# TensorE multiplies zeros in four of its pauses, and the first rows of the attention are scaled in another order

## The reference, cut to what matters

```
x = x + 0.5 * ffn(layernorm(x))       # router, top 2 of 64 experts, plus a shared expert
x = x + attn(layernorm(x))
x = x + 0.5 * ffn(layernorm(x))       # the same weights again

attn(x): n  = ln(x)*g + b
         W1 = gelu(n@h1_w1+b)@h1_w2+b;  W2 = gelu(n@h2_w1+b)@h2_w2+b
         W3 = tril(W1 @ W2^T);          t  = ln(gelu(W3 @ n))*g + b
         out = x + mlp_fm(ln(x + t)*g + b)
```

## Time and profile before

| | us |
|---|---|
| runs | 2206.85, 2216.04, 2218.53 |
| median | 2216.04 |
| profiled execution | 2217.58 |
| its span, first to last instruction | 2215.4 |
| PE busy | 1978.3 (89%) |
| DVE, ACT, POOL busy | 1324.0, 1085.1, 1105.9 |
| TensorE clock granted, mean of the span | 0.965 of full |

### The profile page before, as it was taken

How to read it: one execution, slowest core, us unless ns; L and a number is a source line. 1 busy time by engine, 2 the same in 40 slices (tenths; PEclk the granted TensorE clock), 3 DMA queues, 4 the chain that set the end, 5 groups by cost and what they waited for, 6 DMA issues and landing times.

```text
span 2215.4 us, 32427 instructions
## 1 busy us (share of the span) xinstructions
PE 1978.3 (89%) x11044; PEld 1675.5 (76%) x11044; DVE 1324.0 (60%) x3515; ACT 1085.1 (49%) x1988; POOL 1105.9 (50%) x1202
## 2 busy tenths in 40 slices
PE   6886888779999999999999999999999972888887
PEld 4665788658888888888888878878888862887754
DVE  6996555355576566576576575565565442554467
ACT  6774666434454454454454354444453442555643
POOL 5665666453245545545545645645525316555500
PEclk9998999989999999999999999999999985999999
DMA  8433888792032021121121210110100202888778
GB/s 274 144 105 129 269 272 275 245 301 61 1 96 67 30 95 38 59 95 41 56 89 31 73 43 21 52 39 20 58 10 20 86 10 67 274 274 287 240 250 280
DMA packets 236405, 270.06 MB, mean 122 GB/s; under 512 B 25489, under 2 KB 186322, under 8 KB 236242
## 3 DMA queue, kind: packets, MB, share of 16 engines
q1 hardware_dynamic: 199122, 192.40, 27.7%
q0 software_dynamic: 28672, 67.22, 9.3%
q10 hardware_dynamic: 8448, 8.39, 1.1%
HBM read 150.35 MB, written 117.57 MB: 121 GB/s over the span
## 4 chain that ended last, share of the span: by engine, by line
PE 60%; DVE 8%; issue 5%; ACT 4%; POOL 1%; DMA 1%; another core or an unknown queue 1%; SPq 0%; ACTq 0%; DVEq 0%; POOLq 0%
PE attention_ring L1926 20%; PE attention_acc L1956 13%; PE attention_acc L1946 8%; DVE attention_hid_l L1659 2%; PE attention_work L2016 2%; PE attention_work L1999 2%; PE attention_work L2032 2%; PE attention_work L2036 2%; PE attention_acc L2139 2%; PE attention_ring L2129 2%; PE attention_ring L2165 2%; PE attention_acc L2129 1%; PE attention_work L1914 1%; PE attention_ring L2116 1%; PE attention_work L1973 1%
## 5 line engine op out<-in xcount | busy, mean ns | idle before, releaser
L1659 DVE TENSOR_TENSOR attention_hid_l<-attention_gelu,attention_hid_h 128x512 fp32r<-128x512 f32 x384 | 284.5, 741 | 504.4 <-ACT attention_gelu L1303 320.3
L1300 ACT ACTIVATE attention_hid_h<-attention_ring,home_b 128x512 fp32r<-128x512 f32 x384 | 264.2, 688 | 572.6 <-PE attention_ring L1926 500.0
L1303 ACT ACTIVATE attention_gelu<-attention_ring,home_b 128x512 f32<-128x512 f32 x384 | 261.7, 682 | 0.0
L1956 PE MATMUL attention_acc<-attention_hid_h,home_w_h 128*128 128x512 f32 x512 | 203.9, 398 | 21.0 <-DVE home_room L1685 18.7
L1926 PE MATMUL attention_ring<-attention_n_t_h,home_w_h 128*128 128x512 f32 x512 | 206.0, 402 | 1.4 <-DVE attention_n_t_l L1651 1.4
L1926 PE MATMUL attention_ring<-attention_n_t_l,home_w_h 128*128 128x512 f32 x512 | 201.7, 394 | 0.0
L1926 PE MATMUL attention_ring<-attention_n_t_h,home_w_l 128*128 128x512 f32 x512 | 201.6, 394 | 0.0
L1956 PE MATMUL attention_acc<-attention_hid_l,home_w_h 128*128 128x512 f32 x512 | 200.3, 391 | 0.0
L1956 PE MATMUL attention_acc<-attention_hid_h,home_w_l 128*128 128x512 f32 x512 | 200.2, 391 | 0.0
L1147 POOL DMA_INDIRECT home_room<-expert_rows,routing_slots x128 | 135.9, 1061 | 98.3 <-issue 53.8
L648 POOL DMA_INDIRECT experts_xg<-xn_rows,routing_affine x128 | 141.8, 1108 | 71.9 <-PE experts_ps_t L741 35.3
(11 more groups left out here) (277 smaller groups left out, 5247.1 us busy)
## 6 DMA issues: line engine op xcount, KB each, us to landing
experts_w<-in_L_ffn_w SPq DMA_DIRECT2D x64, 256.0 KB
expert_rows<-experts_y SPq DMA_DIRECT2D x64, 256.0 KB
slot_rows<-const_zeros SPq DMA_DIRECT2D x16, 1024.0 KB
token_rows<-const_zeros SPq DMA_DIRECT2D x16, 1024.0 KB
home_room<-in_L_ffn_w SPq DMA_DIRECT2D x64, 256.0 KB
home_room<-slot_rows SPq DMA_DIRECT2D x64, 256.0 KB
final_y_rows<-token_rows SPq DMA_DIRECT2D x32, 512.0 KB, 7.4
dispatch_x_in<-in_L_attn_x SPq DMA_DIRECT2D x16, 512.0 KB, 7.1
```

What stands on the lines that cost most here:

```text
L1300: act.activation(hid[n % PARTS][0][:, :], ring[n % RING][:, :], ACT.Gelu, bias=b1[:, m, c:c + 1])
L1303: act.activation(gelu[n % GELUS][:, :], ring[n % RING][:, :], ACT.Gelu, bias=b1[:, m, c:c + 1]).then_inc(ring_free, 1)
L1659: dve.tensor_tensor(hid[n % PARTS][1][:, :], gelu[n % GELUS][:, :], hid[n % PARTS][0][:, :].bitcast(fp32), ALU.subtract).then_inc(hid_read ...
L1956: last = pe.matmul(acc[e % 3][:, :], w2[m][wp][:, c, k * P:(k + 1) * P], hid[s][xp][:, :], start=(c == 0 and q == 0), stop=(c == FC - 1 an ...
```

## The change

It has two parts.

**A multiplication of zeros.** A new function issues matmuls of the constant tile (128 columns of it as weights, all 256 as data) into a bank of PSUM whose content nobody needs at that time. PE calls it in four places: 60 times at the start of `experts`, ahead of `turn(0)`; 30 times at the start of the attention, after a new wait for `x_ready` 2; 90 times after the last `down`, ahead of `turn_x`; 165 times after the last placing, ahead of the first slots. The wait of L2142 moves ahead of the 90.

**The start of the attention.** ACT gets one activation with Gelu on 128 single numbers as its first instruction there. DVE makes `n` of group 0 before `z`, now with a wait for `x_scales` ahead of `n_first`. `n_second(0)` no longer waits for `z_ready`, and POOL's `sums` does instead.

```
+def keep_turning(pe, out, zeros, times):
+    for _ in range(times):
+        pe.matmul(out, zeros[:, 0:P], zeros[:, :], start=True, stop=True)
...
@@ experts, tensor
+            keep_turning(pe, ps_y[1][:, 0, :], consts["zeros"], 60)
             turn(0)
             turn(1)
...
@@ attention_to_end, gpsimd, sums(j)
                 pool.wait_ge(n_ready, 8 * (j + 1))
+                pool.wait_ge(z_ready, GT * (j + 1))
...
@@ scalar
+            act.activation(table_in[:, :], consts["partition"][:, :], ACT.Gelu)
...
@@ vector, n_second(j)
-                dve.wait_ge(z_ready, GT * (j + 1))
+                if j:
+                    dve.wait_ge(z_ready, GT * (j + 1))
...
             row_statistics(0)
-            make_z(0)
+            dve.wait_ge(x_scales, 1)
             n_first(0)
             n_second(0)
+            make_z(0)
             turned_lo(0, TURN_M, n_t, 0, n_hi, n_lo)
...
@@ tensor
+            pe.wait_ge(x_ready, 2)
+            keep_turning(pe, acc[2][:, 0:D], consts["zeros"], 30)
             pe.wait_ge(n_ready, 8)
             turn(n_of(0), None, 0)
...
+            pe.wait_ge(ring_free, item(HALVES, FC - 1) + 1)
+            keep_turning(pe, ring[2][:, 0:D], consts["zeros"], 90)
             turn_x(HALVES + 1, (place_in_done, x_turned), (HALVES - 1, KD * (HALVES - 1)))
             router(HALVES + 1)
             place_tiles(HALVES + 1, index_done, GT * HALVES)
+            keep_turning(pe, ring[2][:, 0:D], consts["zeros"], 165)
...
-            pe.wait_ge(ring_free, item(HALVES, FC - 1) + 1)
             pe.wait_ge(acc_free, bank_use(HALVES, H1, 1) + 1)
```

3 lines of the change are left out of this document (2 added, 1 removed).

## The result

The changed kernel took 2221.14 us (median of 20 executions, 2213.74 to 2228.32), the kernel before 2212.78 us beside it (20 executions, 2199.78 to 2226.75). The ratio is 1.0041, with an interval of 1.0027 to 1.0054: 8.4 us slower by the medians, 9 us by the ratio, where 5.1 us faster was forecast. The profiled execution took 2218.34 us, its span is 2216.4 us.

What follows compares the result with a forecast made beforehand. PE, busiest at 89% of the span, was taken as the bound, costly at half clock just behind its pauses. Gains 0.5 + 3.8 + 0.8 + 0 = 5.1 us took 2217.58 to 2212.5, on the median 2211.0; range 2203 to 2219.

Steps and rivals of the forecast that it cites:

- 20.9 us, against 21.66 of pause: Before the second experts: 165 multiplications, 21 cold and 144 warm, fit PE's pause; 0 us gained (1.8 gained to 1.7 lost).
- run 144 multiplications in a row at 0.114 us: Before the second experts: after 21 cold multiplications, the last train's other 144 run warm and take 16.4 us.
- The rival that was slower: All four trains: zeros do not raise the clock, so trains end late; 20.4 us slower, 2236.5 us; chance 0.08.
- Pause 2: Before the attention: train of 30 and new order of n and z start its matmuls sooner and warm; 3.8 us gained.
- the order of `n` and `z`: At the attention's start: z behind n takes four instructions off the path, 1.3 us net, so n is done at 454.4.
- Pause 1: Before the first experts: train of 60 lets the twelve matmuls of gate_up(0) run warm; 0.5 us gained.
- Pause 3: Before the last router: train of 90 speeds the transposes, but the clock falls before the router; 0.8 us gained.
- the clock holds up to the router: Rival: the last router runs warm, 2.6 us gained there, 6.9 to 10.3 in all, 2209.1 to 2205.7; chance 0.30.
- The last train's own gain: At the second experts: first four done some 1.8 us sooner, lost to a longer wait for expert 4's slots; 0.
- The Gelu table: At the attention's start: loading it early is worth 0, as its load was hidden; 0.3 us by the skill's rule.

Runs made afterwards that it cites:

- f1: The changed kernel without its first train of 60; ratio 0.9963 to the kernel before.
- g1: The changed kernel itself, run again in a later set; ratio 0.9980 to the kernel before.
- g2: The changed kernel without its first train of 60, repeated in a later set; ratio 0.9978 to the kernel before.
- h2: The changed kernel itself, run for the third time; ratio 0.9979 to the kernel before.
- g4: The changed kernel with the first train's 60 multiplications moved into the second pause, ahead of its wait; ratio 0.9974 to the kernel before.
- i1: The changed kernel itself, run for the fourth time, on a third chip; ratio 1.0029 to the kernel before.
- f2: The changed kernel without its first and last trains (60 and 165); ratio 0.9980 to the kernel before.
- g3: The kernel before, unchanged, run for its profile; 2151.36 us (one execution).
- f4: The kernel before, unchanged, run for its profile on another chip; 2153.0 us (one execution).
- e1: The changed kernel without its last train of 165; ratio 0.9985 to the kernel before.
- e2: The changed kernel with its last train cut from 165 to 80 multiplications; ratio 1.0007 to the kernel before.
- h3: The changed kernel without its last train of 165, repeated in a later set; ratio 0.9979 to the kernel before.
- e3: The changed kernel with its last train as 82 multiplications of 512 columns in place of 165 of 256; ratio 1.0006 to the kernel before.
- e4: The changed kernel with the train ahead of the experts 200 long in place of 60, and no last train; 2201.5 us (one execution).
- h1: The changed kernel with six 1 MB stores of zeros added to SyncE's queue behind the last tokens' base rows; 2165.58 us (one execution).
- i2: The changed kernel without its first and last trains, on a third chip; ratio 0.9988 to the kernel before.
- f3: The changed kernel without all four trains, keeping the table load and the order of n and z; ratio 0.9984 to the kernel before.
- i3: The changed kernel without its trains of 60, 90 and 165, keeping the 30; ratio 0.9986 to the kernel before.

## Why the prediction was wrong

**The place and the step.** The step that failed is "20.9 us, against 21.66 of pause". Its price of a multiplication was right: 20.4 to 20.6 us were measured in f1, g1, g2 and h2, and 19.6 in g4, where the train came out right. But it rested on 0.8 us of margin and on PE being able to run 144 multiplications in a row at 0.114 us beside GpSimd's indirect stores, which no row of the kernel before showed. It took 37.3 and 37.6 us in the first result and in i1. Where 0 was forecast for this pause, 11.2 us were lost. The ends given for this pause, 1.8 gained and 1.7 lost, were drawn from the clock alone; the end on the other side should have been bounded by a late train. The rival that was slower had the train late for another reason (zeros that do not raise the clock) and priced the cold train at 35.1 us. Its reason was wrong, but its arithmetic of a late last train would have given the size: 13.5 late less 1.95 of wait is 11.5 there, 15.4 late less 4.2 that came back is 11.2 here.

**What was right.** In the sets where nothing holds PE up, the changed kernel came out at 0.9980 and 0.9979; the forecast was 2211.0 / 2216.04 = 0.9977. That the total fits so well is partly luck, since the terms vary by more. Pause 2 was forecast at 3.8 us (2.8 to 4.4) and measured 4.1 in the first profile and in f2, 3.2 in f1, and 2.3 in g1 and g2, which is outside the range: their trains took 6.0 and 5.8 us instead of 5.0, and in g3, against which they are read, the clock rose after 7 of the eighteen matmuls, not after 11 or 12 as in the first profile and f4. Of the order of `n` and `z` 1.3 us were expected off DVE's path, and by itself it measured 1.8 against f4 (1.0 against g3). Pause 1 was forecast at 0.5 us (1.5 to -0.9), and g1 and g2 say 0. In the first result the clock fell again before `gate_up(0)`, which the prediction had taken as warm; in g1 it was warm, and the gain was still lost to a train that ended behind its rows. Pause 3 was forecast at 0.8 (to 2.6). Fifteen profiles have its train. Six of them gained 0.8 (e1, e2, f1, h2, h3, i1), five 1.1 to 1.7 (the first among them), four 2.5 (e3, f2, g1, g2), as the clock fell before, during or behind the router. So the step was right, and the rival "the clock holds up to the router" came true in four of fifteen. The last train's own gain was given back, as forecast: against g3, g1's lead is 2.7 us at the loads, 5.2 at the copy of expert 3's slots and 2.5 at that of expert 4's. The Gelu table was worth nothing that can be seen.

**Why the leads do not add up to the medians.** Up to the attention e1, e2 and e3 run the code of the changed kernel. At the end of the experts they stand 3.2 us (e1) and 1.1 us (e2) ahead of the first profile of the kernel before, and 2.5 us behind it (e3); the changed kernel's own profile stands 5.2 us ahead. Where PE stalls at random, one profile is good to some 3 us per stage. So it is in the first result: the two profiles end 0.9 us apart and the medians 8.4 apart, in part since 5.2 us of the changed kernel's lead were there before the attention began. The sum of the pauses could be read only where PE does not stall.

**What stays open.** Why engines stand still without a releaser in some sets and not in others, on one and the same chip. The slow stretch came only where that state and GpSimd's indirect stores met: e4 had the state without the stores, h1 the stores without the state, and neither had a gap. That it needs both is likely but not shown. It goes by instructions and not by columns (e3). The fetch of instructions is the obvious suspect. The trace lists it as two queues of their own, of which the larger has 91 packets and 1.49 MB, 16 KB each. The Trainium skill (Runtime: NRT & Kernel Launch, "Instruction fetch mechanics") says the same of the size (the smaller queue has packets of 8 KB here), and that the next block comes while the current one runs, so that it is mostly hidden. The trace speaks against a block that is under way too long. The block that was fetched during the last train took 3.2 us in the first result, against about 1.1 on the average of all blocks; but it took 3.0 us in g1 as well, where the train ran without a gap. And it had landed at 1846.5, 2.2 us before the first gap; on neither queue does another packet move until 1880.5, behind the whole train. In e2, e3 and i1 too no packet moves in the gaps. What lies between a fetched block and PE, the trace does not show. A kernel without the indirect stores was not tried in the state that brings the stretch.

**What to keep of the change.** The order of `n` and `z`, and not the first and the last train. With the trains of 30 and 90 (f2, i2) the ratio is 0.9980 where the changed kernel is at 0.9980, and 0.9988 where it is at 1.0029. Without the two (f3) the ratio is 0.9984, and without the 90 (i3) 0.9986, which is within the scatter: the profiles credit these trains with 1 to 5 us together, the times do not show it.

## What to carry to other kernels

A train of idle work has a fixed length, and the wait behind it does not: give it a margin of several microseconds or leave it out, above all where another engine's stores run beside it and where nothing waits for a warm PE afterwards. Price what you add also in the case that it runs at half speed, and use that price as the bad end of the range. Read a gain of the clock in several profiles, for the same train in the same place brought 0.8 us in one and 2.5 in another. And when a gain is some 0.3%, time it in more than one set of runs: the sign of this change was different from set to set, and two profiles side by side told why.

## What the runs showed of the hardware

- One and the same kernel (the one before) took 2193, 2152 and 2156 us in three sets on one chip, 2152 and 2195 on two others, and 2213 in the first result. The slower profiles have idle stretches with no releaser: in the attention of the first one up to 4.4 us on DVE and 4.2 on ACT, and up to 3.1 on PE elsewhere.
- In such a state PE ran 15 to 20 multiplications in 16 to 17 us beside GpSimd's indirect stores, with starts on a grid of 0.70 us.
- Multiplications of nothing but zeros raise the clock: in the first result it was at 1.00 in 210 to 212, towards the end of a train that began at 202.63. It falls again if the train ends well ahead of its data. It then came back 10.3 us into the slots in e2, whose train ended 8.6 us ahead, and 6.3 to 8.0 us into them in ten profiles without the last train.
- After one and the same train of 90 the clock fell before, during or behind the router, which took 3.7, 2.8 to 3.4 or 2.0 us.
- 165 multiplications of 256 columns from a cold start take 19.6 to 20.6 us when nothing holds them up, 90 warm ones 10.00 us (0.111 each).
